# Loops of two attention stages and a layer written out in a token tower

## The reference

```
h = tok(ids)                                   # 16 x 1024 x 64
h = h + linear_attention(layernorm(h))         # 8 heads of 8 channels, elu + 1
h = h + experts(layernorm(h))                  # 64 -> 256, gelu, best of 8 experts
h = h + L1_attn(layernorm(h))                  # 8 heads, full softmax:
#   A = softmax(q k^T / sqrt(8)) over 1024 keys; u = A v;  out = u Wout + bout
h = h + L1_ffn(layernorm(h))                   # 4 heads x 4 experts, causal softmax:
#   scores = q k^T * 4 + causal; att = softmax; out = att v; gates mix the 4 experts;
#   then layer norm, two small matrices, layer norm and a gate over heads
```

## Time and profile before

| | |
|---|---|
| median of 3 runs | 4984.87 us (4984.84 to 4988.16) |
| span of the profiled execution | 4982.3 us; the time of the runs has 2.6 us more around it |
| instructions | 122822 |
| PE | 4651.3 us busy, 93% |
| DVE | 3648.7 us, 73% |
| ACT | 3173.7 us, 64% |
| POOL | 2208.7 us, 44% |

### The profile page before, as it was taken

The page is one execution under the profiler, slowest core; times in us unless marked ns, Lnnn a source line. Parts: engine busy times, 40 slices in busy tenths (PEclk is TensorE's granted clock), DMA queues, the critical chain, the costliest instruction groups (busy, mean ns, idle before and its releaser), DMA issues. The chain is left out here.

```text
span 4982.3 us, 122822 instructions
## 1 busy us (share of the span) xinstructions
PE 4651.3 (93%) x42323; PEld 2070.5 (42%) x42323; DVE 3648.7 (73%) x6356; ACT 3173.7 (64%) x3464; POOL 2208.7 (44%) x2149
## 2 busy tenths in 40 slices
PE   5999979999999999999999979999999999999965
PEld 3444423333333333333333334444444444444433
DVE  4666656666666666666666678888888888888878
ACT  2443426666666666666666648888888888888844
POOL 2233243333332323233333346566666666666656
PEclk9999989999999999999999979999999999999966
DMA  4211100000000000000000000000000000000001
GB/s 101 68 51 51 51 1 2 1 2 1 2 1 2 1 2 1 2 1 2 1 2 1 1 1 3 3 3 3 3 3 3 3 3 3 3 3 3 3 7 27
DMA packets 43766, 52.86 MB, mean 11 GB/s; under 512 B 33416, under 2 KB 33544, under 8 KB 43144
## 3 DMA queue, kind: packets, MB, share of 16 engines
q1 hardware_dynamic: 40440, 44.03, 3.4%
q10 hardware_dynamic: 2704, 0.72, 0.1%
HBM read 39.73 MB, written 4.19 MB: 9 GB/s over the span
## 5 line engine op out<-in xcount | busy, mean ns | idle before, releaser
L1686 DVE TENSOR_REDUCE a_mp<-psum 128x1 f32<-128x512 f32 x2072 | 1325.2, 686 | 674.3 <-PE psum L1563 669.9
L2412 DVE TENSOR_REDUCE f_mp<-psum 128x1 f32<-128x512 f32 (+2 forms) x2352 | 1475.3, 684 | 212.8 <-PE psum L2234 200.0
L1531 ACT ACTIVATE a_prob<-psum,escale 128x1024 f32<-128x1024 f32 x1024 | 1087.0, 1110 | 534.3 <-PE psum L1612 533.9
L2194 ACT ACTIVATE f_prob<-psum,escale_f 128x1024 f32<-128x1024 f32 x1152 | 1247.4, 1112 | 226.2 <-PE psum L2303 109.9
L1620 PE MATMUL psum<-a_prob,a_v 128*64 128x512 f32 x4104 | 993.9, 605 | 0.0
L2048 POOL TENSOR_SCALAR f_hi<-f_raw,part 128x512 f16<-128x512 f32 x324 | 506.5, 1563 | 418.1 <-ACT f_raw L2152 411.8
L2234 PE MATMUL psum<-f_kf,f_qf 64*128 64x512 f16 (+2 forms) x3658 | 657.7, 309 | 35.5 <-DVE f_mp L2412 24.8
L1451 POOL TENSOR_TENSOR a_u<-a_og,a_inv 128x512 f32<-128x512 f32 x129 | 134.4, 1042 | 1166.1 <-DVE a_inv L1701 1166.1
L2324 PE MATMUL psum<-f_prob,f_vh 128*32 128x512 f32 (+3 forms) x6144 | 614.7, 495 | 6.3 <-DVE f_oc L2434 5.6
L2303 PE MATMUL psum<-f_qf,f_kf 64*128 64x512 f16 (+3 forms) x3074 | 505.6, 329 | 39.9 <-ACT f_og L2157 18.2
L1620 PEld LDWEIGHTS psum<-a_prob,a_v 128*64 128x64 f32 x4104 | 248.9, 136 | 504.9 <-issue 498.7
(11 more groups left out here) (440 smaller groups left out, 6749.0 us busy)
## 6 DMA issues: line engine op xcount, KB each, us to landing
idx<-in_itok_BS_dram SPq DMA_DIRECT2D x36, 512.0 KB, 6.3
idx<-in_itok_BS_dram SPq DMA_DIRECT2D x54, 256.0 KB, 7.6
idx<-in_x_dram SPq DMA_DIRECT2D x18, 256.0 KB, 3.7
a_qh<-a_rowT SPq DMA_DIRECT2D x258, 1.0 KB
out_dram<-h SPq DMA_DIRECT2D x16, 256.0 KB, 2.6
f_qf<-f_rowT SPq DMA_DIRECT2D x130, 4.0 KB, 1.7
wd<-in_L_ffn_Wd_dram SPq DMA_DIRECT2D x2, 256.0 KB
bd<-in_L_ffn_bd_dram ACTq DMA_DIRECT2D x16, 2.0 KB
```

The costliest lines, as they stand in the source:

```text
L1531: act.activation(prob[:, part], k.psum[:, pair:pair + 2].rearrange("p b n -> p (b n)"), ACT.Exp, scale=k.escale[:]).then_inc(s.read, 1)
L1686: dve.tensor_reduce(mp[:, tg % 2, t + 4 * r, c:c + 1], bank_of(j + r), X, ALU.max)\
L2194: act.activation(prob[:, u % NPF], k.psum[:, pair:pair + 2], ACT.Exp, scale=k.escale_f[:])\
L2412: dve.tensor_reduce(side[:, at[0]:at[-1] + 1:step], bank_of(j + r)[:, 0:len(at) * width].rearrange("p (a b) -> p a b", b=width), X, ALU.ma ...
```

## The change

In `layer0`, `attention1` and `feedforward1` the loops of POOL, ACT, PE and DVE become loops of Python, so that the program holds every turn's instructions one after the other: 7 turns in `layer0`, 8 in each attention stage. `i` is then a number, and with it every value that is waited for and every address. SP's loops stay, and so do those of `finish1`. Nothing else is edited; there are twelve places like these three:

```diff
@@ layer0, PE
-                with pe.Fori(0, PAIRS_ - 1) as i:
+                for i in range(PAIRS_ - 1):
                     for n in range(L_SLOTS):
                         slot(n, i + 1, i)
@@ attention1, PE
-                with pe.Fori(0, NB // 2) as i:
+                for i in range(NB // 2):
                     for x in range(AROUND):
                         G = i * AROUND + x
@@ feedforward1, ACT
-                with act.Fori(0, NB // 2) as i:
+                for i in range(NB // 2):
                     for x in range(ROUND):
                         G = i * ROUND + x
```

More of the change, by code:

```diff
@@ L755, in _ @@
                 pool.sem_inc(E["h"], 8)
-                with pool.Fori(0, PAIRS_ - 1) as i:
+                for i in range(PAIRS_ - 1):
                     back(i)
@@ L851, in _ @@
                     slot(n, 0, None)
-                with act.Fori(0, PAIRS_ - 1) as i:
+                for i in range(PAIRS_ - 1):
                     for n in range(L_SLOTS):
@@ L1216, in _ @@
                 steps = start + 17
-                with dve.Fori(0, PAIRS_ - 1) as i:
+                for i in range(PAIRS_ - 1):
                     link = Link(dve, s.d, i * steps + start)
@@ L1476, in _ @@
                 split_q(1, 1, 3)
-                with pool.Fori(0, NB // 2) as i:
+                for i in range(NB // 2):
                     for x in range(AROUND):
@@ L1719, in _ @@
                     read_out(0, -1, j, kind, of + 1, part)
-                with dve.Fori(0, NB // 2) as i:
+                for i in range(NB // 2):
                     for x in range(AROUND):
```

## The result

The changed kernel takes 4935.6 us (median of 4 runs, 4933.9 to 4936.7). The kernel before, run beside it on the same chip, takes 4986.5 us (4 runs, 4984.8 to 4991.0). The ratio is 0.9898, 95% interval 0.9884 to 0.9911: 1.0% faster. 4935.3 was forecast. The profiled span falls from 4982.3 to 4934.4 us, by 47.9.

What follows compares the result with a forecast made beforehand. PE was taken to bound layer 0 and both attention stages. The span of 4982.3 us less 49.0 for attention jumps and 0.6 for layer 0, with 2.6 around it, gave 4935.3 us; own range 4925 to 4945, outer range 4918 to 4960.

Steps and rivals of the forecast that it cites:

- the price of a turn's end: Attention stages: whole turns against halves without a jump give 2.5 us a jump in the first, 4.5 in the second.
- Point 1: PE's loops of both attention stages written out: 14 stalls go, 17.3 + 31.7 = 49.0 us.
- rival (a): Turn borders in attention: only the idle gap comes back, or table loads stay; about 4952 us, chance 0.11.
- The clock dip: Second attention stage: PE's clock at 0.50 for 2.4 us after the 3.0 us gap, counted within the 49.0 us.
- Point 2: ACT's attention loops: 7 of 8 table loads go in each stage, 18 us of ACT, already inside the 49.0.
- The rival priced there: ACT's table loads stay while PE's branch goes: up to 18 us of the 49 would stay.
- Point 3: DVE's and GpSimd's loops: their branches lie under PE's stall, so nothing beside it.
- Point 4: Layer 0: 6 PE jumps of 0.22 us, between 0 and 1.3 us gained, 0.6 taken; fetching taken as 0.
- Rival (c): Layer 0: straight code stalls on fetching, 78 us lost, 5013 us in all; chance 0.03.
- Point 5: Register work of loop-dependent waits: gain at most 16 us, loss at most 10 us, taken as 0.
- Rival (b): Second attention stage, ring PE-ACT-PE: register steps were on the path, 65.6 us gained, 4919 us; chance 0.07.
- Rival (d): PE's 3.4 us come with each turn, not from fetching a jump target, and stay; about 4983 us, chance 0.04.

Runs made afterwards that it cites:

- run 3: Kernel before with only layer 0's loops written out, on its four engines: 5015.3 us, ratio 1.0060.
- run 4: Changed kernel with ACT's two attention loops kept as loops: 4969.1 us, ratio 0.9963.
- run 2: Kernel before with the attention loops of ACT, DVE and GpSimd written out, PE's kept: 4985.6 us, ratio 0.9998.
- run 9: Changed kernel with GpSimd's two attention loops kept as loops: 4938.5 us, ratio 0.9909.
- run 8: Kernel before with two turns a body in the attention loops of four engines, 3 jumps a stage for 7: 4966.7 us, ratio 0.9958.
- run 10: Kernel before with layer 0's loop holding three turns a body on each engine: 5035.0 us, one execution.
- run 6: Kernel before with 107 idle semaphore instructions on PE ahead of the second attention stage: 5012.4 us, ratio 1.0048.
- run 7: Kernel before with layer 0 written out and 149 idle semaphore instructions on PE ahead of the second attention stage: 5006.0 us, ratio 1.0042.

## Why the prediction was right

The step that carries the forecast, the price of a turn's end taken from the half without a jump, was right. That the time was met to 0.3 us is luck in part: the jumps gave 1.7 us less than forecast, and the kernel before came out 1.6 us above the 4984.9 that the sum began with.

Point 1, the jumps: 49.0 us forecast, 47.3 measured. A turn came out 0.17 and 0.09 us longer than the 265.4 and 222.0 that the halves without a jump gave. Turn borders keep a small cost of their own: the border head takes 16.7 us where the same head in mid-turn takes 16.3, the border unit 27.85 for 27.42. The skipped PSUM bank stands there, but no run took it away, so its part is not shown. Of rival (a) this much is true.

The clock dip was rightly counted with the gap. It is gone with it, it is longer where the gap is doubled (6.8 us at half clock in run 3, where a single gap has 3.4; the 2.4 us of the earlier trace rows were the part of it in that window), and L2303 and L2234 wait no longer than inside a turn.

Point 2, ACT's table loads, went, as forecast. The reason given was incomplete. It read ACT's 1.28 us load ending just before PE's restart, and missed ACT's own jump of 2.6 us in front of it. The rival priced there ("if they stayed while the branch went", up to 18 us) would have been 34 us with the jump (run 4 against the change). The sum was not touched, because the change removes both.

Point 3, DVE's and GpSimd's loops at nothing: true with PE's loops in place (run 2), and true of GpSimd's in any case (run 9). DVE's alone are worth 14 us once PE's and ACT's are gone (4952.7 less 4938.5; 18 by the turns of the two traces). On the engines themselves these jumps last 2.7 to 3.1 us (DVE) and 0.2 to 2.7 us (GpSimd) in the kernel before. "Nothing beside it" was a statement on the order of the stalls, not on their size. The change had to be made whole to bring the 47 us: 0 of it with PE's loops left, a third with PE's alone.

Point 4, layer 0: no cost for 17 packets more of code. From its first pair to the first head of attention it takes 591.3 us for 593.1; 1.2 of this is one pair of 75.5 us that came out at 74.4. The 0.6 forecast and what is left of the span, 47.9 - 47.3, agree by luck: layer 0's first pair starts 3.2 us later in the changed kernel's trace (145.3 for 142.1). Rival (c), which put the whole at 5013, was wrong in its mechanism. Its count of 210 PE instructions to a block left the register steps out; with them a turn of the first stage has 4265, some 256 to a block. Yet layer 0 written out alone does cost 28 us (run 3), by moving the later loops. The prediction had no such step, and needed none, as the change leaves no dear jump whose target could lie badly.

Point 5, register work at nothing: the units inside a turn of the second stage are 27.06, 27.57 and 28.66 us, where they were 27.05, 27.66 and 28.74. That is 0.3 us a turn, some 2 us over the stage. Neither bound (16 us less, 10 us more) was approached. Rival (b) is out.

Rival (d) is out: in run 8 the turns that end without a jump lose all but 0.3 and 0.6 us of the excess, and run 10 makes a jump of PE dear in layer 0 that was cheap.

The Trainium skill ("Runtime: NRT & Kernel Launch", Instruction fetch mechanics) has crossings into the next block mostly hidden and a taken branch out of what is held waiting for its fetch. The runs agree on the second, at 3.3 to 4.6 us on PE. On the first they agree in straight code and differ right behind a jump: there a crossing 8 to 42 instructions behind the target took 1.4 to 3.1 us more.

The same section of the Trainium skill gives what an engine holds: 2048 instructions on PE and 512 on the others, in blocks of 256. On PE the runs agree: 1486 is cheap and 2229 dear. On the others a body below 512 was not enough. Cheap were 230 (GpSimd) and 306 (DVE); dear, at 2.4 us and more, were 328 and 458 (GpSimd), 457 (DVE), 519 and 535 (ACT), 655 and 714 (DVE). 365 (GpSimd) was dear in all runs but run 10, where other code ahead of it had moved it, and cheap there. So where a body lies in its blocks seems to count beside its size; no run varied that alone on these engines.

## What to carry to other kernels

Where the engines' backward jumps lie beside each other, a turn's end costs what the one that is latest for the bounding engine costs, so price and remove them on all engines together. Removing one engine's can show nothing, and that says nothing about the rest. Where they lie apart, as PE's and DVE's in layer 0 of run 10, each can be paid. Look for the jump in the branch record on PE, and on ACT, DVE and GpSimd in the gap behind a short branch record. Where a long loop has to stay, count where its target lies in the code: moving the second stage's target cost 16 us in run 6, and moving it back gave 22 us (1609.1 in run 3, 1586.6 in run 7), with nothing changed in what the loop does. Then look at the granted clock behind each jump before a difference of 2 us in a turn is put down to anything else.

## What the runs showed of the hardware

- A backward jump on PE: 0.2 us up to a body of 1486 instructions, 3.3 to 4.6 us from 2229 on. On ACT 2.3 to 2.9 us with bodies of 519 and 535, not in the branch's record (45 ns). On DVE 0.2 to 0.3 us with 306, 2.7 to 3.6 with 655 and 714. On GpSimd 0.2 us with 230, 2.4 to 2.8 with 365 in all runs but run 10, and 0.2 there.
- A block that ends 8 to 42 instructions behind the target of PE's jump gave a second stall of 1.4 to 3.1 us. With it the excess of a turn is 7 to 10 us, for 4.4 in the second stage and 2.3 in the first.
- DVE's jump beside id loads of 133 GB/s took 6.4 us (run 10).
- The granted clock was 0.50, the 1.2 GHz level, for 3.4 us (3406.1 to 3409.5, kernel before) at one gap of 3.0 us, and for 6.8 us (3417.7 to 3424.5) after two gaps of 3.0 and 2.3 us. In run 7 three of the seven gaps of 2.9 to 3.3 us in the second stage had no such stretch. After single gaps of 1.6 to 2.3 us in the first stage it stayed at 1.00 in most cases and fell for 3.4 us in some: in 2 of 7 in run 6 (gaps of 2.11 and 2.12 us) and in 3 of 7 in run 7 (1.95 to 2.11 us), though a gap of 2.27 us in run 7 had none. Such a turn took some 2 us more.
- Straight code in layer 0 was fetched at no visible cost, 19 packets beside id loads that move 51 GB/s on average, in bursts.
- 107 and 149 idle semaphore steps on PE delayed the next stage by 5.8 and 12.1 us, 54 to 81 ns each.
